# Row shifts of a one-channel convolution on TensorE, a 528-byte pitch in front of transposes, and 2 KB output stores

## The reference

```python
def c1(t): return conv(t, w1 (1x9x128x1), 'SAME') + b1    # 9 taps along a row, 128 channels to 1
t = relu(c1(x))                                           # one channel, 256 x 256
y = concat([x[:, :1], x[:, 1:] + t[:, :-1]], axis=1)      # t of the row above
u = relu(c1(y))
z_main = u + roll(y, 1, axis=1)
z = concat([z_main[:, :H-2], u[:, H-1:H] + y[:, H-2:H-1], y[:, H-1:H]], axis=1)
```

```python
gate_A, gate_B = sigmoid(conv7x7(x, gate_A_kernel)), sigmoid(conv7x7(x, gate_B_kernel))   # depthwise, circular
a_t, b_t = a_spatial * gate_A, conv7x7(x, B_kernel) * gate_B
log_h = scan over T = 8 equal steps of (a_t, b_t), through softplus and logaddexp
out = exp(log_h[-1]) @ W_out + b_out
```

## Time and profile before

| | |
|---|---|
| time, median of 3 runs | 4745.81 us (4656.36, 4745.81, 4747.08) |
| the profiled execution | 4665.72 us, span 4663.7 us |
| busy share of the span | PE 93%, DVE 73%, ACT 61%, POOL 45% |
| `one_channel_part` in the span | 3402.8 to 3466.3 us |
| `depthwise_layer` without convolutions (block 7's patches) | 4557 to 4664 us |
| granted TensorE clock, mean | 0.964 of full speed |

### The profile page before, as it was taken

How to read it: one execution, slowest core, us unless ns; L and a number is a source line. 1 busy time by engine, 2 the same in 40 slices (tenths; PEclk the granted TensorE clock), 3 DMA queues, 4 the chain that set the end, 5 groups by cost and what they waited for, 6 DMA issues and landing times. The chain is left out here.

```text
span 4663.7 us, 108212 instructions
## 1 busy us (share of the span) xinstructions
PE 4324.7 (93%) x35238; PEld 3310.7 (71%) x35238; DVE 3407.1 (73%) x10109; ACT 2858.4 (61%) x7950; POOL 2102.6 (45%) x1792
## 2 busy tenths in 40 slices
PE   5999999999999999877999989999739997999995
PEld 5777777777777777646677757777414447999995
DVE  7888888888888888663666656666339993667665
ACT  0888888888888888513333333333317882666664
POOL 0777777777777777513233313333016650222222
PEclk8999999999999999899999989999869998999997
DMA  7222222222222222385222222221847887999994
GB/s 317 69 77 77 80 77 79 78 76 80 77 76 80 77 77 80 130 292 183 68 73 71 72 83 71 73 71 64 301 164 254 295 279 254 278 286 294 288 294 113
DMA packets 726507, 679.49 MB, mean 146 GB/s; under 512 B 59029, under 2 KB 609172, under 8 KB 717399
## 3 DMA queue, kind: packets, MB, share of 16 engines
q1 hardware_dynamic: 710507, 643.38, 45.0%
q10 hardware_dynamic: 11645, 15.81, 1.0%
q0 software_dynamic: 3808, 13.47, 0.7%
HBM read 473.14 MB, written 199.29 MB: 144 GB/s over the span
## 5 line engine op out<-in xcount | busy, mean ns | idle before, releaser
L325 POOL TENSOR_TENSOR at_bias<-at_tri,at_mask 128x1024 f32<-128x1024 f32 x512 | 1204.6, 2375 | 115.7 <-DMA at_mask<-in_L_conv_mask_bias_dram 111.1
L465 ACT ACTIVATE at_probs<-at_neg_s,at_neg_max 128x256 f32<-128x256 f32 x2048 | 1012.9, 504 | 0.5 <-DVE at_neg_max L509 0.5
L509 DVE CUSTOM_DVE_ANT_0 at_neg_s<-at_p_s,at_bias 128x256 f32<-128x256 f32 x2048 | 761.9, 419 | 17.9 <-PE at_p_s L367 3.6
L1008 ACT ACTIVATE ml_h<-ml_p_turns,l_b 128x512 f32<-128x512 f32 x384 | 263.9, 687 | 608.1 <-PE ml_p_turns L967 608.1
L380 PE MATMUL at_p_t<-all_ident,at_probs 128*128 128x128 f32 x4096 | 614.1, 273 | 1.1 <-DVE at_probs_t L517 0.6
L976 PEld LDWEIGHTS ml_p<-l_w1s,ml_h 128*128 128x128 f32 x4096 | 471.9, 192 | 52.7 <-issue 52.7
L380 PEld LDWEIGHTS at_p_t<-all_ident,at_probs 128*128 128x128 f32 x4096 | 487.3, 141 | 28.3 <-ACT at_probs L465 2.6
L967 PE MATMUL ml_p_turns<-ml_h,l_w 128*128 128x512 f32 x1024 | 486.2, 598 | 2.3 <-DVE ml_h L1041 2.3
L976 PE MATMUL ml_p<-l_w1s,ml_h 128*128 128x128 f32 x4096 | 484.6, 277 | 0.8 <-issue 0.8
L1109 POOL TENSOR_TENSOR ml_x2t<-ml_z,ml_xb 128x512 f32<-128x512 f32 x128 | 163.3, 1276 | 678.3 <-DVE ml_z L1075 678.3
L2036 POOL TENSOR_TENSOR dw_room<-dw_room,all_b_plain 128x512 f32<-128x512 f32 x128 | 175.6, 1372 | 598.5 <-DMA dw_room<-x3t 598.5
(11 more groups left out here) (232 smaller groups left out, 9225.7 us busy)
## 6 DMA issues: line engine op xcount, KB each, us to landing
dw_xw<-planes SPq DMA_DIRECT2D x128, 528.0 KB, 4.7
dw_wts<-patch_w SPq DMA_DIRECT2D x128, 512.0 KB, 6.0
planes<-pw_plane SPq DMA_DIRECT2D x128, 264.0 KB, 3.1
in_xs<-in_x_dram SPq DMA_DIRECT2D x32, 1024.0 KB, 7.7
at_xs<-in_x_dram SPq DMA_DIRECT2D x256, 128.0 KB, 2.3
at_kvs<-in_L_conv_kv_x_dram SPq DMA_DIRECT2D x256, 128.0 KB, 2.3
at_mask<-in_L_conv_mask_bias_dram SPq DMA_DIRECT2D x256, 128.0 KB, 3.2
x<-at_x1s SPq DMA_DIRECT2D x256, 128.0 KB, 1.8
```

Of the source, the lines that this page charges most:

```text
L325: pool.tensor_tensor(bias[:, n % 2, part], tri[:, part], mask[:, n % 4].unsqueeze(1).broadcast_to((128, 4, COLS)), ALU.add).then_inc(maske ...
L465: e = act.activation(probs[:, h, qh, :], neg_s[:, n % 2, h, qh, :], ACT.Exp, bias=neg_max[:, n % 2, i:i + 1], scale=-1.0, accum_out=sums[: ...
L509: t = dve.tensor_tensor_reduce(neg_s[:, n % 2, h, qh, :], p_s[h][:, qh, :], bias[:, n % 2, i, :], -1.0, 3.0e38, ALU.add, ALU.min, neg_max[ ...
L1008: act.activation(h1[:, b, :], bank_of(hidden_use(t, b))[:, :], ACT.Relu, bias=b0[:, b:b + 1]).then_inc(relu_act, 1)
```

## The change

There are four edits.

1. `spread_taps` takes the 64 spots of a patch in the order of columns (`ox, oy` instead of `oy, ox`); `copy_pair` is as before.
2. `one_channel_part` no longer moves `t` and `u` through DRAM. A constant `row_moves` (128 x 1536 floats, 768 KB, an input made on the host like the identity) is loaded behind the taps; PE multiplies `t` by it into `p_above` (PSUM, margins cleared by DVE), and `t` and `u` into `p_tau`. DVE's 18 additions read PSUM, and its last instruction copies `p_tau`. POOL clears only margins, and SP no longer waits for it. ACT's store of `tw` waits until the taps and `row_moves` are in SBUF.
3. In `depthwise_layer` the lines of `raw` get 4 floats more: 132 floats, 528 bytes.
4. Each transpose writes its 128 columns into `p_turn` in runs of 4 floats, 16 floats apart, so that `gate`, `bt` and `soft` are flat, `hid` is [SPOTS // 4, PX, 4], and a unit's sum has 4 neighbouring columns of a position's channels in one partition. The write into `hid` becomes two instructions of 128 x 16 x 16 with runs of 64 bytes; the residual is loaded to 128 partitions instead of 32 at a time; and the unit's store is one DMA with runs of 2 KB where there were four DMAs with runs of 512 bytes.

SP's list in `one_channel_part` before: `convs` is the DRAM scratch for `t` and `u`.

A unit's four stores became one; the residual loads are as many as before. The diff, cut:

```diff
-                    oy, ox = divmod(spot + i, PATCH)
+                    ox, oy = divmod(spot + i, PATCH)
...
-            sp.wait_ge(cleared, 4)
             for half in range(2):
                 sp.dma_start(ts[:, half, :, side:side + COLS],
                              taps.rearrange("j (h p w) -> h p j w", p=128, w=COLS)[half]).then_inc(taps_loaded, 16)
-            sp.wait_ge(t_made, 1)
-            sp.dma_start(t_d.rearrange("(h p) w -> p h w", p=128), t[:, :, :]).then_inc(t_stored, 16)
-            sp.wait_ge(t_stored, 16)
-            place(sp, above[:, :, side:side + COLS], t_d, 1, ROWS - 1, 0, above_loaded)
-            n = place(sp, t_of, t_d, 0, 1, ROWS - 2, tau_loaded)
-            n += place(sp, t_of, t_d, 2, ROWS - 4, 0, tau_loaded)
-            n += place(sp, t_of, t_d, ROWS - 2, 2, ROWS - 3, tau_loaded)
-            sp.wait_ge(u_made, 1)
-            sp.dma_start(u_d.rearrange("(h p) w -> p h w", p=128), u[:, :, :]).then_inc(u_stored, 16)
-            sp.wait_ge(u_stored, 16)
-            n += place(sp, u_of, u_d, 0, ROWS - 2, 0, tau_loaded)
-            n += place(sp, u_of, u_d, ROWS - 2, 1, ROWS - 1, tau_loaded)
-            assert n == 7
+            sp.dma_start(moves[:, :, :, :].rearrange("p a h r -> p (a h) r"), row_moves).then_inc(moves_loaded, 16)
             sp.wait_ge(tau_made, 1)
-            sp.dma_start(tau.rearrange("(h p w) -> p h w", p=128, w=COLS), u_of[:, :, :]).then_inc(tau_stored, 16)
+            sp.dma_start(tau.rearrange("(h p w) -> p h w", p=128, w=COLS), tau_s[:, :, :]).then_inc(tau_stored, 16)
...
+            act.wait_ge(taps_loaded, 32)
+            act.wait_ge(moves_loaded, 16)
...
+            def move(out, kind, src, to, halves, first, last):
+                for i, h in enumerate(halves):
+                    mm = pe.matmul(out, moves[:, kind, h, to * 128:(to + 1) * 128], src[:, h, :],
+                                   start=first and i == 0, stop=last and i == len(halves) - 1)
+                return mm
+
+            pe.wait_ge(moves_loaded, 16)
+            pe.wait_ge(t_made, 1)
+            for to in range(2):
+                move(p_above[to][:, side:side + COLS], 0, t, to, range(to + 1), True, True).then_inc(above_made, 1)
+            for to in range(2):
+                if to == 1:
+                    pe.wait_ge(u_made, 1)
+                    move(p_tau[:, 0, :], 2, u, 0, (0,), False, True)
+                move(p_tau[:, to, :], 1, t, to, range(2), True, False)
+            move(p_tau[:, 1, :], 2, u, 1, (1,), False, True).then_inc(tau_summed, 1)
...
-            pool.memset(ts[:, :, :, :], 0.0).then_inc(cleared, 1)
-            pool.memset(above[:, :, :], 0.0).then_inc(cleared, 1)
             pool.memset(ones[:, :], 1.0).then_inc(cleared, 1)
-            pool.memset(u_of[:, :, :], 0.0)
-            pool.memset(t_of[:, :, :], 0.0).then_inc(cleared, 1)
+            for first in (0, side + COLS):
+                pool.memset(ts[:, :, :, first:first + side], 0.0).then_inc(cleared, 1)
...
-            dve.wait_ge(above_loaded, 32)
+            dve.wait_ge(above_made, 2)
...
-                    a = dve.scalar_tensor_tensor(out=acc[:, half], in0=above[:, half, j:j + COLS],
+                    a = dve.scalar_tensor_tensor(out=acc[:, half], in0=p_above[half][:, j:j + COLS],
...
-            dve.wait_ge(tau_loaded, 16 * 7)
-            dve.tensor_tensor(u_of[:, :, :], u_of[:, :, :], t_of[:, :, :], ALU.add).then_inc(tau_made, 1)
+            dve.wait_ge(tau_summed, 1)
+            dve.tensor_copy(tau_s[:, :, :], p_tau[:, :, :]).then_inc(tau_made, 1)
...
-        raw = m.sb("raw", [128, CH, BLOCK_PY * PX])
+        raw = m.sb("raw", [128, CH, BLOCK_PY * PX + 4])
...
-        hid = m.sb("hid", [128, 2, SPOTS, PX])
+        hid = m.sb("hid", [128, 2, SPOTS // 4, PX, 4])
...
-        p_turn = [m.ps(f"p_turn{i}", [128, PATCH, 2 * SPOTS]) for i in range(2)]
+        p_turn = [m.ps(f"p_turn{i}", [128, 2, 2, SPOTS // 4, 4, 4]) for i in range(2)]
+        by_patch = [t[:, :, :, :, :, :].rearrange("p h f s a y -> p h f (s a y)") for t in p_turn]
...
-                    sp.dma_start(xr[d * PX:(d + 1) * PX, w % 4], cells[(1 - x) * SHIFT + d][:, y:y + 4]).then_inc(r_loaded[w % 4], 16)
+                    sp.dma_start(xr[:, w % 4, d], cells[(1 - x) * SHIFT + d][:, y:y + 4]).then_inc(r_loaded[w % 4], 16)
...
-                for d in range(4):
-                    sp.dma_start(out[0, r * PATCH + y:r * PATCH + y + 4].rearrange("y (a d) c -> d a y c", d=PATCH)[x + d],
-                                 outs[d * PX:(d + 1) * PX, w % 4]).then_inc(stored[w % 4], 16)
+                cells = out[0, r * PATCH + y:r * PATCH + y + 4].rearrange("y (a d) c -> a y d c", d=PATCH)
+                sp.dma_start(cells[:, :, x:x + 4].rearrange("a y d c -> a y (d c)"),
+                             outs[:, w % 4].rearrange("p d c -> p (d c)")).then_inc(stored[w % 4], 16)
...
-                    cells = raw[:, patch, :] if u // units % 2 else raw[:, :, patch]
-                    mm = pe.transpose(p_turn[u % 2][:, i, :], cells, ident[:, :])
+                    cells = raw[:, patch, 0:CH] if u // units % 2 else raw[:, :, patch]
+                    places = p_turn[u % 2][:, i // 4, :, :, i % 4].rearrange("p f s y -> p (f s) y")
+                    mm = pe.transpose(places, cells, ident[:, :])
...
-                    mm = pe.matmul(p_out[w % 2][:, i, :], hid[:, r % 2, spot:spot + 4].rearrange("p s a -> p (s a)"),
+                    mm = pe.matmul(p_out[w % 2][:, i, :], hid[:, r % 2, (x + i) * 2 + y].rearrange("p a y -> p (a y)"),
...
-                dve.scalar_tensor_tensor(out=hid[:, r % 2, :, x:x + PATCH].rearrange("p s a -> p a s"), in0=bt[:, u % 3],
-                                         scalar=0.0, in1=soft[:, u % 2], op0=ALU.max, op1=ALU.add).then_inc(hid_made, 1)
+                for half in range(2):
+                    part, at = slice(half * BANK // 2, (half + 1) * BANK // 2), x + half * 4
+                    done = dve.scalar_tensor_tensor(out=hid[:, r % 2, :, at:at + 4].rearrange("p s a y -> p s (a y)"),
+                                                    in0=bt[:, u % 3, part].rearrange("p (s n) -> p s n", n=16), scalar=0.0,
+                                                    in1=soft[:, u % 2, part].rearrange("p (s n) -> p s n", n=16),
+                                                    op0=ALU.max, op1=ALU.add)
+                done.then_inc(hid_made, 1)
...
-                    dve.wait_ge(stored[w % 4], 64 * (w // 4))
+                    dve.wait_ge(stored[w % 4], 16 * (w // 4))
...
```

More of the change, by code:

```diff
@@ L1300, in _, with one_channel_part @@
             dve.tensor_tensor(b_plain, brow[:, :], p_b, ALU.add)
-def one_channel_part(nc, taps, w1, b1, scratch, tau, tw, patch_w):
+def one_channel_part(nc, taps, w1, b1, row_moves, tau, tw, patch_w):
     side = TAPS // 2
     wide = COLS + 2 * side
-    t_d, u_d = scratch[0], scratch[1]
     with ExitStack() as ctx:
         m = Scope(nc, ctx, "oc")
+        moves = m.sb("moves", [128, 3, 2, ROWS])
         w = m.sb("w", [128, TAPS])
@@ L1331, in one_channel_part @@
         block = ctx.enter_context(nc.Block())
[L1333 to L1341, removed]
         @block.sync
@@ L1752, in depthwise_layer @@
         og_final = m.sb("og_final", [KTAPS, CH])
[L1753 removed]
+        og_room = hid[:, :, :, :, :].rearrange("p r s a y -> p (r s a y)")
         og_taken = 0
@@ L1892, in turn_origin @@
                 for i in range(2):
-                    mm = pe.transpose(p_turn[0][:, i, :], og_xs[:, i, :], ident[:, :])
+                    mm = pe.transpose(og_turn[:, i, :], og_xs[:, i, :], ident[:, :])
                 mm.then_inc(og_turned, 1)
@@ L1925, in copy_raw @@
             else:
-                done = copy(raw[:, c:c + 4, :], p_conv[g % 2][:, :, :])
+                done = copy(raw[:, c:c + 4, 0:BLOCK_PY * PX], p_conv[g % 2][:, :, :])
             done.then_inc(copied, 1)
@@ L2090, in origin_window @@
                     chained(dve.tensor_copy(og_win[:, :, first:first + k],
-                                            p_turn[0][:, part, base:base + span * k].rearrange("p (y d) -> p y d", d=k)))
+                                            og_turn[:, part, base:base + span * k].rearrange("p (y d) -> p y d", d=k)))
                 chained(dve.tensor_reduce(og_sum, og_kern[:, 1, :], mybir.AxisListType.X, ALU.add))
@@ L2181, in build @@
           c_w1, c_b1, c_w2, c_b2, a_kernel, b_kernel, gate_a, gate_b, w_out, b_out,
-          identity, group_mean, forward, inverse_rows, inverse_cols, selector, out):
+          identity, group_mean, forward, inverse_rows, inverse_cols, selector, row_moves, out):
     def scratch(name, shape):
@@ L2194, in build @@
     taps_d = scratch("taps_d", [TAPS, TOKENS])
-    convs = [scratch(f"convs{a}", [ROWS, COLS]) for a in range(2)]
     tau = scratch("tau", [TOKENS])
@@ L2231, in build @@
                                        kept, tw, taps, ksum[:, :], w_plain[:, :], b_plain[:, :])
```

(15 more changed lines are left out.)

36 lines of the change are left out of this document (20 added, 16 removed).

## The result

The changed kernel takes 4619.38 us (median of 4 runs, 4611.99 to 4621.55) against 4656 to 4658 us for the runs of before that compare with it. The ratio is 0.9917, with a 95% interval of 0.9893 to 0.994: 28 to 50 us less. Forecast were 4632 us, 34 less than the profiled execution's 4665.7. Of the terms, one was put at nothing and is 13 us, and one was too large, as the trace shows.

What follows compares the result with a forecast made beforehand. PE was taken to bound the depthwise blocks, DMA and waits the one-channel stage, SP the program's end. Savings of 23 + 10 + 1 = 34 us from 4665.7 gave 4632 us, range 4605 to 4728.

Steps and rivals of the forecast that it cites:

- The one-channel stage: Whole stage up to the next stage's first DMA: -23 us, with -17 and -26 as ends.
- Taps: One-channel stage: taps, loaded ahead of the `tw` store without waiting for POOL, land at 3416.1 instead of 3431.6, -15.5 us.
- Matmuls for `above`: One-channel stage: three matmuls with hand-overs take 2.6 us instead of a 10.33 us wait, -7.7 us.
- Behind `u`: One-channel stage: four matmuls and hand-over, 2.1 and 0.6 us, replace 4.74 us of DMA, -2.0 us.
- the store, not the chain, comes last by a little: One-channel stage's end: `tw` store ends at 3441.5, next DMA at 3442.5; the chain alone would give 3441.1.
- The pitch of 528 bytes: Depthwise blocks, strided transposes: lines of 528 bytes leave the price of single-float reads unchanged, 0 us.
- the rival: Depthwise blocks: odd pitch makes strided transposes as cheap as whole lines, 19 us more saved, 4613 us; chance 0.33.
- The program's end: Last units' loads and stores: one store for four shortens SP's list, -10 us (-7 to -12).
- four rounds of loads cost SP 4 x 1.88 us: Program's end: SP's last residual loads, with three stores of 0.52 us, take 9.1 us back to back.
- Softplus: Write into `hid`: two instructions of 456 ns for one of 1139, 0.23 us less a unit; -1 us in all.
- The runs of four in PSUM: Transposes' strided PSUM write in runs of 16 bytes costs nothing, 0 us.
- The rival that they lengthen every transpose: Depthwise blocks: strided PSUM write adds up to 87 ns to each of 1024 transposes, 89 us, 4721 us; chance 0.10.

Runs made afterwards that it cites:

- the order: Kernel before with only ACT's wait added, so `tw` is stored once the taps are in SBUF; `t` and `u` still through DRAM: stage 62.4 us.
- the rest of the new part: Changed kernel with the store of `tw` issued at the start of the one-channel stage again, without ACT's wait: stage 51.4 us.
- the changed kernel's second profile: Changed kernel run again unaltered, beside a run with the last residual loads on ACT: 4620.9 us, ratio 0.9917.

## Why the prediction came out right, and where it did not

*The one-channel stage* was forecast at -23 and is -25.4. Taps -15.5, measured -17.9 (10.9 us from the stage's start to the first addition, for 28.8). Matmuls for `above` -7.7, measured -7.2. Behind `u` -2.0, measured -0.9: the four matmuls with their hand-overs took 3.87 us, not 2.7. The additions from PSUM, taken as unchanged, are. The chain of these, -25.2, is what came. The taps gained 2.4 us more than forecast; w1's gather, which was taken to hold them up until it lands after 5.2 us, lands in 2.2 now. The step "the store, not the chain, comes last by a little" failed: the store begins 13.8 us after the stage's start and ends 1.1 us before `tau` has landed, so the 2 us allowed for it were not needed. The store beside it did not hold the chain up: DMA is busy to the end of the stage (share 0.91 from 3413.6 to 3440 us), and the next DMA follows `tau`'s issue by 4.1 us, for 3.5 before. That the moves must leave DMA before the store may stand beside them is shown by the two halves: 1.1 us for the order, 12.1 for the rest of the new part (8.3 of it the moves), 25.4 for both.

*The pitch of 528 bytes* was taken at **0** and is -13.2 us; this step failed. It held that single floats 128 and 512 bytes apart cost DVE about the same, so the price is one for each float from another place. That compared two powers of two with one another, and on another engine, as the text itself said. The trace had no row that could speak for 0, and the rival was the other reading of the same rows: it asked for 19 us, 0.30 a unit, and got 0.21. What it did not say is that the 13 us depend on SP. A chance of 0.33 went to this rival, and the time came out nearer to it than to the forecast.

*The program's end* was taken at **-10**. The last eight sums and what follows them took 30.0 us before and 24.0 after: -6.0. The step that four rounds of loads cost SP 4 x 1.88 us failed: a round takes 2.5 to 3.1 us now, so the loads and not the stores set the pace. The bracket (-7 to -12) named the risk and was too narrow.

*Softplus* at -1 can't be told. The stretch from the last convolution to the first of the last eight sums fell by 9.0 us between the two profiles, but it varies: it was 68.9 to 76.6 us in five kernels with the old layout and 66.9 to 71.9 in eight executions with the new (78.5 with four stores). The granted clock there was 0.78 before and 0.91 after, but it is not the whole of it: the changed kernel's second profile took 70.0 us at 0.78, and two runs with the old layout 72.5 and 73.0 at 0.77. The working behind the -1 failed: the two instructions were put at 456 ns each and take 645 in this stretch, for one of 1182. What got shorter is the magnitude ahead of them, 692 ns for 930. In the blocks DVE gained nothing either: two instructions of 656 ns for one of 1134, and the magnitude 698 ns for 841.

*The runs of four in PSUM* at 0 are 0. The rival that they lengthen every transpose is refuted by the whole lines: 0.87 us and 141 ns in both kernels. On the rule that PSUM access that isn't contiguous slows matmuls, of the Trainium skill's "PSUM — Partial Sum Buffer", section Specifications, the trace does not agree for runs of 16 bytes at a step of 64.

So 34 us were forecast out of 23 + 10 + 1, and the profiles have 25.4 + 13.2 + 6.0 and 9.0 whose cause is open, while the timed runs show 28 to 50 in all. That 34 lies within them is in part luck: a term of 13 was missing, 4 us too many at the end made up for a part of it, and by the timed runs the whole change is worth less than by the two profiles. "PE never waits for DMA" was right of the kernel before and hid that SP had some 0.2 us a unit to spare: issues and gaps of 5.27 us on the average in a round of 5.49.

## What to carry to other kernels

Before taking time out of the bounding engine, sum the issue times of the queue that feeds it per unit: with the pitch alone SP's 5.33 us left no room in PE's 5.35, and 13 us of faster transposes became 5 in the trace and nothing that the timed runs show. Changes can be worth much more together than apart (1.1 and 12.1 give 25.4; 4.9 and 0.2 give 13.2), and one that looks like a detail may carry the rest: the single store is what keeps the new layout from losing 2%. Where transposes read single floats from lines of 512 bytes, as here, another pitch is worth a trial, at 4 to 16 bytes a line.

## What the runs showed of the hardware that I had not expected

- Weight loads that pick one float from each of 128 lines take 254 ns at a pitch of 512 bytes, 220 at 516, 205 at 520 and 209 at 528, against 141 for a contiguous line.
- The same DMA takes longer to issue by what stands around it: the windows' load 0.37 us at the stage's start in every kernel, later 0.43 (median) in the old layout and 0.59 in the new, though its own form is the same. Why the new loads and stores take 0.60 and the old 0.43 stays open; with a quarter of the partitions, though not in a row, the new loads still take 0.60.
